# One-core attention and feed-forward kernel: transpositions moved inside accumulations, the Q and K projections in another order, and the first group's K filled from SBUF

## The reference, cut to what matters

```python
q = proj(LN(x), W_Q, b_Q); k = proj(ctx, W_K, b_K); v = proj(ctx, W_V, b_V)
attn = softmax(q k^T / sqrt(32)); out = attn v          # 16 heads, 512 x 512 scores each
```

## Time and profile before

| | |
|---|---|
| median of 3 runs | 1621.0 us (1618.87 to 1624.04) |
| profiled execution, own time | 1623.71 us |
| its span, first to last instruction | 1621.9 us |
| PE / DVE / ACT / POOL busy | 1477.0 / 1226.8 / 875.9 / 890.9 us |
| mean granted TensorE clock | 0.958 of 2.4 GHz |
| attention phase ends, next phase begins | 872.86 us |

### The profile page before, as it was taken

One profiled execution on the slowest core, in us unless ns is written; L12 is line 12 of the kernel. 1 busy time (PEld: TensorE's weight loads), 2 busy tenths in 40 slices (PEclk: granted clock), 3 DMA queues, 4 the chain that ended last, 5 costly groups with the idle time before them and its releaser, 6 DMA issues. The chain is left out here.

```text
span 1621.9 us, 24716 instructions
## 1 busy us (share of the span) xinstructions
PE 1477.0 (91%) x6993; PEld 937.9 (58%) x6993; DVE 1226.8 (76%) x2135; ACT 875.9 (54%) x1433; POOL 890.9 (55%) x1148
## 2 busy tenths in 40 slices
PE   5699999999999889899784999999999968999997
PEld 3466666556565566655532455555555447887885
DVE  4867677777868677677662788888888848999986
ACT  4156666666565556555453555555555535555552
POOL 3166676585675757656462343343333316777775
PEclk9899999999999989999878999999999989999998
DMA  6757849485694865937941344444444653556522
GB/s 201 227 163 211 258 150 273 143 249 161 185 277 128 229 190 176 289 108 226 251 115 55 95 114 109 109 116 107 107 107 109 190 146 120 167 165 203 166 86 62
DMA packets 252172, 265.32 MB, mean 164 GB/s; under 512 B 139932, under 2 KB 162984, under 8 KB 247720
## 3 DMA queue, kind: packets, MB, share of 16 engines
q1 hardware_dynamic: 252072, 264.14, 57.4%
HBM read 149.50 MB, written 82.87 MB: 143 GB/s over the span
## 5 line engine op out<-in xcount | busy, mean ns | idle before, releaser
L724 ACT ACTIVATE a_probs<-a_sc 128x512 f32<-128x512 f32 x512 | 300.5, 595 | 288.5 <-PE a_sc L608 284.7
L843 DVE TENSOR_REDUCE a_negmax<-a_mx 128x1 f32<-128x512 f32 x512 | 339.0, 675 | 108.1 <-PE a_mx L591 107.3
L938 POOL TENSOR_TENSOR a_acc<-a_acc,a_probs 128x512 f32<-128x512 f32 x248 | 311.6, 1285 | 11.1 <-ACT a_probs L724 9.7
L938 POOL TENSOR_TENSOR a_acc<-a_probs 128x512 f32<-128x512 f32 x124 | 156.9, 1285 | 247.9 <-ACT a_probs L724 247.0
L591 PE MATMUL a_mx<-a_stack 96*128 96x512 f32 x512 | 231.0, 451 | 40.3 <-DVE a_negmax L843 22.3
L1089 PE MATMUL bank<-wcode,b_xq 128*128 128x512 bf16 x1024 | 229.3, 383 | 11.1 <-DMA b_xq<-b_xcode 11.1
L608 PE MATMUL a_sc<-a_stack 97*128 97x512 f32 x512 | 217.7, 427 | 21.0 <-DMA a_stack<-a_mrow 19.5
L1089 PEld LDWEIGHTS bank<-wcode,b_xq 128*128 128x128 bf16 x1024 | 100.5, 98 | 135.0 <-DMA b_xq<-b_xcode 12.5
L854 DVE RECIPROCAL a_attn<-a_den 128x128 f32<-128x128 f32 x128 | 120.8, 947 | 71.1 <-PE a_den L646 58.6
L591 PEld LDWEIGHTS a_mx<-a_stack 96*128 96x128 f32 x512 | 103.1, 201 | 114.4 <-DVE a_negmax L843 55.0
L1127 ACT ACTIVATE b_sig<-bank,b_tok 128x512 f32<-128x512 f32 x128 | 87.4, 683 | 94.0 <-PE bank L1089 91.9
(11 more groups left out here) (165 smaller groups left out, 2637.0 us busy)
## 6 DMA issues: line engine op xcount, KB each, us to landing
a_stack<-spill SPq DMA_DIRECT2D x192, 256.0 KB, 6.8
spill<-k_part SPq DMA_DIRECT2D x64, 512.0 KB, 3.5
ctx_t<-k_wo SPq DMA_DIRECT2D x16, 1024.0 KB, 9.8
c_ct<-ctx_t SPq DMA_DIRECT2D x8, 2048.0 KB, 7.9
a_stage<-in_x_dram SPq DMA_DIRECT2D x32, 256.0 KB, 5.1
a_stage<-in_ctx_dram SPq DMA_DIRECT2D x32, 256.0 KB, 3.1
a_wsum<-in_L_ffn_w_gate_dram SPq DMA_DIRECT2D x8, 1024.0 KB, 6.1
attn_t<-a_attn SPq DMA_DIRECT2D x32, 256.0 KB, 4.6
```

The lines of the kernel that those rows point to most:

```text
L724: nc.scalar.activation(probs[:, k, j, :], sc[i % 2][:], ACT.Exp, scale=SCALE).then_inc(exp_done, 1)
L843: nc.vector.tensor_reduce(negmax[:, g % 2, j, t:t + 1], mx[i % 2][:], axis=AX.X, op=ALU.max, negate=True).then_inc(mx_done, 1)
L938: nc.gpsimd.tensor_tensor(acc[:, j], probs[:, 0, j] if k == 1 else acc[:, j], probs[:, k, j], ALU.add)\
```

## The change

The change does six things in the attention phase.

1. The PSUM bank of each user is a written table (`BANK`) and no longer given in turn; `Turns.wait_free` looks back for the last user of the same bank. A transposition stands on the other bank than the accumulation around it.
2. The table of times: the four transpositions of x move into the accumulations of V (`tx_at` -14.5 to -3.7), those of the context into the accumulations of Q of the groups 0 and 1 (`tc_at` 2 to 11.2), and V's pieces are 0.9 slots apart.
3. The projections are ordered Q0, Q1, K0, K1, Q2, K2, Q3, K3 (`ORDER`, `RANK`), where they were Q0, K0, Q1, K1, ...
4. The columns of the Q and K weights (and the biases) are permuted once, at the split of the weights, so that a partition of `part` is (row r, head j). A fill then reads four neighbouring rows as one run of 8 KB where it read four runs of 2 KB.
5. K of group 0 (`DIRECT`) is not spilled: its fill goes from `part` in SBUF straight to `stack`. ACT's next write of `part`'s K waits for that fill.
6. The units of feed-forward weights are in the groups 3, 0 and 1 instead of 2, 3 and 0.

```diff
-        n, back = self.turn[key] - len(self.banks), 0
+        n, back = self.turn[key] - 1, 0
...
-            if not isinstance(it, int) or 0 <= it - back + shift < self.batches:
+            if self.chosen[who] == self.chosen[key] and (not isinstance(it, int) or 0 <= it - back + shift < self.batches):
...
-            n -= len(self.banks)
+            n -= 1
...
-    CODE_IN = {n: k for k, n in enumerate((14, 15, 16, 18, 19, 20, 22, 23, 24, 26, 27, 28))}
+    CODE_IN = {n: k for k, n in enumerate((14, 15, 16, 17, 19, 20, 21, 23, 24, 25, 27, 28))}
...
-        tx_at, tc_at = (0, 1.5, 3, 4.5), (10.8, 12.3, 13.8, 15.3)
...
+        tx_at, tc_at = (-14.5, -10.7, -7.2, -3.7), (2, 7, 9.7, 11.2)
+        v_at = [3.6 * i + 0.9 * c for i in range(T) for c in range(C)]
+        ORDER = ((0, Q), (1, Q), (0, K), (1, K), (2, Q), (2, K), (3, Q), (3, K))
...
+        fill_at = {(0, Q): 13, (0, K): 19, (1, Q): 32, (1, K): 37, (2, Q): 44.5, (2, K): 49.5, (3, Q): 52, (3, K): 56}
+        DIRECT = (0, K)
...
-                    elif name == "spill":
+                    elif name == "spill" and args != DIRECT:
...
-                            sp.dma_start(stack[DH * n:DH * (n + 1), g, side].bitcast(F32),
-                                         spill[g, side, h].rearrange("(j r) s -> r j s", j=J))\
-                                .then_inc(stacked[g][side], 16)
+                            src = part[:, side, h].bitcast(F32) if args == DIRECT else spill[g, side, h].rearrange("(r j) s -> r j s", j=J)
+                            sp.dma_start(stack[DH * n:DH * (n + 1), g, side].bitcast(F32), src).then_inc(stacked[g][side], 16)
...
+                        if side == K and g == DIRECT[0] + 1:
+                            wait_count(act, stacked[g - 1][side], it, shift, 1, 1, 48)
```

More of the change, by code:

```diff
@@ L345, in attention_phase @@
                 for c in range(C):
-                    ck.add(ahead(qk_at[g, side] + 1.15 * c), 3, "qk", g, side, c)
-                ck.add(ahead(qk_at[g, side] + 1.15 * (C - 1)) + at["spill"], 9, "spill", g, side)
+                    ck.add(ahead(qk_at[g, side][c]), 3, "qk", g, side, c)
+                ck.add(ahead(qk_at[g, side][C - 1]) + at["spill"], 9, "spill", g, side)
                 ck.add(ahead(fill_at[g, side]), 9, "fill", g, side)
@@ L406, in attention_phase, with spills @@
                 users.append((shift, (name, *args[:-1])))
-        turns = Turns(work, users, NB, read_out)
+        turns = Turns(work, users, NB, read_out, BANK)
+        def spills(g, side):
+            return (G - 1, g) if side == K else (G, g + 1)
         def stage_wait(engine, it, shift, i):
@@ L653, in split_weight @@
                     act.wait_ge(w_loaded[n], 16)
-                    nc.scalar.activation(w["qkv"[n]][:, :, HI, :], probs[:, n], ACT.Copy).then_inc(w_hi, 1)
+                    to, at_n = permuted(n, HI)
+                    nc.scalar.activation(to, at_n, ACT.Copy).then_inc(w_hi, 1)
                 def small_tables():
@@ L666, in put_biases @@
                     act.wait_ge(bias_turned, 1)
-                    nc.scalar.activation(bias[:].rearrange("p n g -> p (n g)"), den[:, 0:3 * G], ACT.Copy).then_inc(bias_done, 1)
-                    act.wait_ge(bias_done, 1)
+                    flat = bias[:].rearrange("p n g -> p (n g)")
+                    nc.scalar.activation(flat[:, 0:2 * G], den[:, 3 * G:5 * G], ACT.Copy).then_inc(bias_done, 1)
+                    nc.scalar.activation(flat[:, 2 * G:3 * G], den[:, 2 * G:3 * G], ACT.Copy).then_inc(bias_done, 1)
+                    act.wait_ge(bias_done, 2)
                 def window(it, shift, name, args):
@@ L688, in window @@
                         g, side, _ = args
-                        wait_count(act, qk_full, it, shift, 2 * G, 2 * g + side + 1)
-                        wait_count(act, spilled[side], it, shift, G, g, 16)
+                        wait_count(act, qk_full, it, shift, 2 * G, RANK[g, side] + 1)
+                        if side == K and g == DIRECT[0] + 1:
+                            wait_count(act, stacked[g - 1][side], it, shift, 1, 1, 48)
+                        else:
+                            per, count = spills(g, side)
+                            wait_count(act, spilled[side], it, shift, per, max(count - 1, 0), 16)
                         nc.scalar.activation(part[:, side, HI, :], turns.bank("qk", g, side)[:], ACT.Identity,
@@ L703, in window @@
                             split_weight(0)
+                        if it + shift == 0 and i == T - 1:
+                            act.wait_ge(bias_loaded, 48)
+                            nc.scalar.activation(bpart[:].rearrange("n (r j) -> n r j", j=J), brow[:].rearrange("n (j r) -> n r j", j=J),
+                                                 ACT.Copy).then_inc(bias_put, 1)
                     elif name == "v" and args[1] == C - 1:
```

57 lines of the change are left out of this document (36 added, 21 removed).

## The result

The changed kernel takes 1641.7 us (median of 15 runs, 1624.9 to 1649.5) against 1624.0 for the kernel before (15 runs, 1618.9 to 1630.1): ratio 1.0099, 95% interval 1.0082 to 1.0116. It is 1% slower where I had predicted 2% faster. The profiled execution has a span of 1639.6 us and a mean granted clock of 0.948.

A forecast was written before the change was run, and what follows sets the result against it. It took PE's pace in group 0, POOL's additions as second limit, and waits with a falling clock as the bound. Clean batches -6.4, batches with units -26.0, first stretch +1: -31.4, so 1590 us, range 1573 to 1613.

The forecast's parts named there:

- the direct fill of group 0 skips spill and landing ...: these waits go: First max of group 0: seven issue waits for K, 7.4 us, go; in clean batches already counted in the 95.1 us.
- The rival by the buffer `part`: ACT stalls writing Q1 and K1 into `part` until earlier DMAs land, 1 to 4.4 us each; over 1626 us; chance 0.10.
- The same for Q: Part of that rival: ACT may write Q1 only when Q0's spill landed, taken at 4.4 us a batch.
- Balance of the groups: Groups 1, 2, 3, 0 of a clean batch at 23.8, 22.0, 22.0, 25.2 us: 2.1 less a batch, 6.4 in three.
- Order of SP's queue: First score's waits for the row of maxima in batches with units: 7.0 of 7.7 us go.
- the step on the clock: Batches with units lose 10.8 us more to a lowered clock than clean ones; only 0.8 a batch stays.
- Batches with units, 26.0 less: The four batches with feed-forward units take 95.7 us each, 381.2 in all against 407.2; bounds 10 and 31 less.
- My 1.0 us a batch for DVE in group 1: Units moved into group 1 cost DVE 3.4 us there, close to the group's time; 1.0 us a batch taken.
- The K1 fill: Four issue waits of the first max for K of group 1 in batches with units, 5.3 us; half taken as gone.
- 8 KB runs: Longer runs in the fills, costed at nothing; bounds 0 and 2.6 us.
- First stretch, +1 taken: Time to the first den: more tiles and the permuted split against a skipped spill; +1 us, bounds -3 and +4.
- The last batch: No change, 0 us: its 8.5 us of waits stay because the four DMA transpositions around them stay in place.

The follow-up runs named there:

- E1: The changed kernel with K of group 0 spilled through DRAM like the others, no direct fill; all else as changed: 1603.7 us.
- E2: The changed kernel without direct fill and without the permutation (2 KB runs in the fills): 1600.8 us.
- E5: The changed kernel, direct fill kept, with Q of group 2 produced between K of group 0 and K of group 1: 1606.4 us.
- E8: The kernel before with SP's queue alone changed: fills of group 2 at 44.5 and 49.5, units and their loads in the new places: 1611.7 us.
- E10: E2 with K1's fill ahead of a spill and a store, and two of the last batch's four DMA transpositions behind the row of maxima: 1586.7 us.
- E4: The kernel before with the permutation and the direct fill of K of group 0, old order: 1632.3 us.
- E3: The kernel before with the permutation alone (permuted split of two weights, fills in 8 KB runs): 1634.9 us.
- E9: E8 with the permutation added (permuted split of two weights, fills in 8 KB runs): 1622.7 us.
- E6: The same kernel as E2, run and profiled again to see its spread: one run, 1603.4 us.

## Why the prediction was wrong

Den-to-den sums of the profiles (us): first den; three clean batches; four with units.

| | first den | clean | with units |
|---|---|---|---|
| before | 100.8 | 286.2 | 407.2 |
| after | 109.3 | 298.9 | 400.8 |
| E1, K0 spilled | 104.1 | 281.3 | 382.2 |
| E2, nor permuted | 103.6 | 282.8 | 384.2 |
| E5, Q2 before K1 | 109.3 | 284.8 | 380.7 |
| E8, before with the new queue | 97.2 | 286.4 | 396.7 |
| E10 | 105.2 | 284.1 | 374.3 |

- **The step that failed: "the direct fill of group 0 skips spill and landing ...: these waits go".** The sum has no term for what the direct fill costs: ACT's next write of K into `part`, K1, must wait until the fill has landed. Measured, ACT waits 3.5 us there in each of the seven batches and 6.7 in the first stretch. Taking the direct fill out (E1) shortens the batches by 36.2 us and the first stretch by 5.2, more than the 32 that the batches were to gain. The step's other half, the gain, failed too. The seven issue waits for K0 went in E1 and E2 as well, with K0 spilled: the new table did it (K0 is ready earlier, and its fill stands at 19 instead of 25), and in the old order the direct fill took about 3 us of them (E4).
- **The rival by the buffer `part` had the place right and the odds wrong.** It put the third DMA's issue 5.9 us behind den and K1 complete at 8.3. Measured: all three issued by 241.6, 6.1 behind the den of 235.45; ACT came to K1 at 244.3, 8.9 behind it. Between a landing of 3.5 us, the spill's, and 6.8, the fill's, the measured one is 5.6 at the median, and that gave 3.4 us of stall. I had argued for the short end, since in group 1 the DMA share is 0.34. That was the wrong group: K0's last piece, and with it the fill, stands behind the den that opens group 2, where the earlier trace rows has 0.73. In the changed kernel it runs there alone, and it is slow even so (below). The rival also had no clock in it: 3.5 us of wait cost 5.2, if group 1's part is counted. With that it stands at the 5 us from which I had said it decides. 0.10 was far too little for a wait that the diff writes out (`wait_count(act, stacked[g - 1][side], ...)`) behind a transfer whose landing no row bounded under 3.5.
- **The same for Q had next to no price in the batches.** The rival's 8.8 us a batch took 4.4 for Q1 behind Q0's spill. The changed kernel shows such a wait once in the batches, 1.4 us; in the first stretch it is 4.48 us in E2.
- **Balance of the groups: right.** 23.8, 22.0, 22.0 and 25.2 predicted; 23.77, 21.98, 22.16 and 25.62 measured once ACT no longer stands (E1). A clean batch takes 93.5, not 93.0, for group 0's 0.4.
- **Order of SP's queue: right, too small.** I took 7.0 us; in E8 the waits of 7.6 are gone and their groups are 11.8 shorter, at a clock of 1.00 in all four where two had 0.94. I had the clock's part in the step on the clock.
- **Batches with units, 26.0 less: 25.0 in E1, 23.0 in E2.** My 1.0 us a batch for DVE in group 1 was not needed (23.80 us in E10 with units, 23.78 in a clean batch). The K1 fill, of which I took half as gone, got worse (8.6 us in four waits, holds 5.3) and went when it was moved in the queue (E10).
- **8 KB runs: nothing gained.** Fills land 5.4 us behind issue with 8 KB runs (E1) and 5.1 with 2 KB (E2). The Trainium skill, "DMA: Bandwidth & Descriptors", Specifications, has 512 B as enough for line rate. By that rule the longer runs bring nothing, and these traces agree. The permutation costs 11.1 us in the old order (E3, E9), and 2.9 in the new, which is not clear of the scatter (E2), where I had 0 to 2.
- **First stretch, +1 taken, bounds -3 and +4: +8.5.** 5.2 are the direct fill (109.3 in the changed kernel and in E5, 103.6 to 105.2 in the runs of the new order without it); the new order leaves 2.8 to 3.3. First stretches differ as much elsewhere (103.6 and 104.9 in two runs of one kernel, E2 and E6; 97.2 in E8, 100.8 before), so I don't split it further. The split itself was in the trace of before only as 1.91 and 2.29 us; permuted it takes 3.8 on both engines.
- **The last batch: 0 taken, 2.9 more up to the end, and it is not the direct fill's:** with K0 spilled (E1) it is 4.9 more. The last batch itself, up to the next phase's first matmul, takes 4.6 us more in the changed kernel and 2.8 in E1. The later phases, whose program is the same everywhere, take 741.5 to 745.9 us from run to run. Of the 4.6, 1.7 are the score's longer wait for the last row of maxima (10.2 against 8.5); the rest stays open.

Not tried: a buffer of its own for K0, 4 KB more in each partition, which would show the direct fill with no order around it.

## What to carry to other kernels

When a transfer reads a buffer in place instead of a copy, ask who writes the buffer next and how soon: price that wait by the slowest landing that the trace shows, and add the clock that falls behind it (here 3.5 us of wait a batch cost 4.3 in its own group, and up to 5.2 with the group before). If the wait is real, another order of the writers can be as good as taking the transfer out (E5, E1). And an in-order DMA queue is worth reading row by row: two moves of fills and units in it were worth 11 us (E8), two more 14 (E10), with no engine doing anything less.

## What the runs showed of the hardware

The direct fill from SBUF is slow with no traffic beside it. Window of the changed kernel while its three DMAs run and no other (here the last two columns count, DMA share and GB/s):

```profile
240.50:247.50 7.00, 5.39 (x21) 3.63 (x20) 4.99 (x8) 1.92 (x4) 3.78 (x3) 1.00 0.80 114
```

The DMA engines are 0.80 busy and move 114 GB/s; in group 3, with spills, fills and loads from DRAM side by side, 0.93 busy give 265 GB/s. So in this kernel a quiet DMA window did not make the transfer land sooner. Which property of the transfer makes it slow is not shown. The direct fills' row from 100 to 800 us (count, KB each, median us to landing):

```profile
a_stack<-k_part SPq DMA_DIRECT2D x21, 256.0 KB, 5.6
```

A weight split of 128 x 2048 with permuted columns took 3.76 and 3.85 us on ScalarE and 3.75 and 3.83 on VectorE, against 1.91 and 2.29 in order. And the same group can run at either pace. Behind the first window, group 1 kept to 23.8 us at a clock of 1.00 in two of six batches of the changed kernel (25.3 at 0.93 in the other four), in four of six of E1 and E2 each, and in five of six of E5 and E10 each. The two groups 1 of a clean batch compared above, 25.32 and 23.77 us, have the same instructions and the same wait of their own, 1.3 us. It is more often slow where group 2 has the long wait, but not only there.
